# Query, key and value products in three 16-bit passes, one copy and one subtraction moved to GpSimd, new order lists, and products without a reader at both ends

## The reference

```python
x = L0_attn_x                                # (8, 512, 256) float32
mod = (silu(L0_c) @ L0_wmod).reshape(8, 6, 1, -1)
sa, ca, ga, sb, cb, gb = ...                 # ga, gb: absolute value at least 0.25
h = layernorm(x) * (1 + ca) + sa
qkv = h @ w_qkv                              # 16 heads of 16
q = elu(rope(q) * 16**-0.25) + 1;  k the same
kv += k[:, None] * v;  ks += k               # scan over the 512 positions
out = (q @ kv) / max(q . ks, 1e-6)
x = x + ga * (out @ w_out)
h = layernorm(x) * (1 + cb) + sb
probs = softmax(h @ router_w.T);  the top 2 of 8 experts, weights made to sum to 1
x = x + gb * sum_e cw_e * (gelu(h @ w1_e) @ w2_e)
```

## Time and profile before

| | us |
|---|---|
| median of three runs (761.94 to 768.41) | 763.54 |
| the profiled execution | 765.42 |
| its span | 763.6 |
| busy in the span: PE, DVE, ACT, POOL | 710.8, 624.6, 567.0, 500.7 |
| mean granted TensorE clock | 0.96 |

### The profile page before, as it was taken

One profiled execution on the slowest core, in us unless ns is written; L12 is line 12 of the kernel. 1 busy time (PEld: TensorE's weight loads), 2 busy tenths in 40 slices (PEclk: granted clock), 3 DMA queues, 4 the chain that ended last, 5 costly groups with the idle time before them and its releaser, 6 DMA issues.

```text
span 763.6 us, 24900 instructions
## 1 busy us (share of the span) xinstructions
PE 710.8 (93%) x8105; PEld 545.1 (71%) x8105; DVE 624.6 (82%) x1494; ACT 567.0 (74%) x1108; POOL 500.7 (66%) x535
## 2 busy tenths in 40 slices
...
GB/s 225 133 62 158 116 150 121 137 139 112 140 113 142 115 128 99 50 28 65 56 76 72 71 71 73 71 78 71 78 69 78 68 77 72 76 70 76 70 21 1
DMA packets 52854, 69.26 MB, mean 91 GB/s; under 512 B 8864, under 2 KB 44080, under 8 KB 52736
## 3 DMA queue, kind: packets, MB, share of 16 engines
...
...
## 4 chain that ended last, share of the span: by engine, by line
PE 55%; POOL 19%; issue 13%; DVE 2%; ACT 2%; DMA 1%; POOLq 0%; ACTq 0%; DVEq 0%
PE hidden L1484 17%; PE bank L1502 16%; PE hidden L1486 8%; PE bank L1504 8%; POOL h L902 4%; POOL kst L941 4%; POOL qst L939 3%; PE bank L1319 2%; POOL rstd L895 2%; POOL kst L932 2%; PE bank L1336 2%; POOL am L921 1%; POOL mod_b L987 1%; POOL ra L946 1%; PE hidden L1319 1%
## 5 line engine op out<-in xcount | busy, mean ns | idle before, releaser
L1484 PE MATMUL hidden<-qstT,w1hi_k 128*128 128x256 f16 x1136 | 197.7, 274 | 0.7 <-DVE qstT L782 0.7
L1486 PE MATMUL hidden<-qstT,w1lo_k 128*128 128x128 f16 x1136 | 193.3, 220 | 0.0
L1502 PE MATMUL bank<-w,amhi 128*128 x568 | 188.4, 379 | 0.1
L1504 PE MATMUL bank<-w,amlo 128*128 x568 | 154.8, 273 | 0.0
L1035 POOL DMA_INDIRECT out_dram<-x,si x71 | 115.5, 1627 | 39.5 <-issue 24.6
L818 DVE TENSOR_TENSOR amlo<-am,amhi 128x512 f16<-128x512 f32 x142 | 98.3, 692 | 49.0 <-ACT am L1195 48.6
L1484 PEld LDWEIGHTS hidden<-qstT,w1hi_k 128*128 x1136 | 111.6, 98 | 13.8 <-issue 1.2
L1486 PEld LDWEIGHTS hidden<-qstT,w1lo_k 128*128 x1136 | 111.6, 98 | 0.5 <-issue 0.2
L1336 PE MATMUL bank<-wq,hT 128*128 128x256 f32 (+1 forms) x256 | 99.4, 513 | 4.2 <-DVE hT L550 2.9
L1502 PEld LDWEIGHTS bank<-w,amhi 128*128 128x128 f16 x568 | 55.6, 98 | 59.9 <-issue 0.4
L1048 ACT ACTIVATE feat<-hidden 128x512 f32<-128x512 f32 x71 | 42.4, 597 | 61.9 <-PE hidden L1486 61.9
...
## 6 DMA issues: line engine op xcount, KB each, us to landing
...
```

Source lines behind the costliest of these rows:

```text
L1484: t.matmul(dst.rearrange("p (q n) -> p q n", q=2), w1s[0][k][g][:, w_], both, start=(k == 0), stop=False)
L1486: last = t.matmul(dst[:, P:2 * P], w1s[1][k][g][:, w_], both[:, 0, :], start=False, stop=(k == KT - 1))
L1502: t.matmul(y[:, :], ghi[:, m.p, c_m], w2s[mt // 2][:, bass.ds(w_, 2 * D)], start=(mt == 0), stop=False)
L1504: last = t.matmul(y[:, D:2 * D], glo[:, m.p, c_m], w2s[mt // 2][:, bass.ds(w_, D)], start=False, stop=(mt == MT - 1))
```

## The change

- `product16` makes queries, keys and values of chunks 3 to 31 from 16-bit halves: for each half of the depth, high rows by high weights, high rows by low weights, low rows by high weights, six products in place of two float32 ones. Chunks 0 to 2 (`PLAIN = 3`) still go by float32, from `wq_raw`, which lies in the second half of tiles for expert weights that are filled later.
- New works for that: `wqh` (ACT, two copies of 128x768) and `wql` (DVE, two) split the weights once; `hh` (ACT) and `hl` (POOL) split the rows of each chunk. The weights are scaled by 64 and the tables of the rotation are left as they were: chunks 0 to 2 get the 64 in `rope`, the others lose it in `vhi` and `vlo`. `vlo` is a `scalar_tensor_tensor` now. The tile `hT` exists once, no longer twice.
- `shq` goes from ACT to POOL, and `slo` is one instruction of 128x512 in place of two: both stacks lie in one tile `stacks`, and the quarter low by low is zero, set once.
- `mv`, `rstd` and `nb` exist twice, so `rs` no longer waits for `nb`, `xn` and `xn2` of the step before; `var` is gone.
- All lists are new. `warm` (two products of the identity with itself) stands nine times in PE's step 1 and three times in its step 5, and `fill` (the same, after the last state is read) twenty times in PE's closing list. The closing lists begin at step 26, not 27.

```diff
-Q_SCALE = WS * float(HD ** -0.25)
+Q_SCALE = float(HD ** -0.25)
-ORDER_POOL = (("h2", 6), ("rs", 0), ("wb", 5), ("shk", 2), ("slo", 2), ("xm2", 5), ("R", 1))
+ORDER_POOL = (("h2", 6), ("rs", 0), ("shq", 2), ("shk", 2), ("slo", 2), ("wb", 4), ("hl", 0), ("R", 1), ("xm2", 5))
...
+PLAIN = 3
...
+        wq16 = wq[:, :, :].bitcast(F16).rearrange("p k n -> p (k n)").rearrange("p (k c n) -> p k c n", k=KT, c=2)
...
-        mv = sb("mv", [P, 2, 2])
-        var = sb("var", [P, 2])
-        rstd = sb("rstd", [P, 2])
-        nb = sb("nb", [P, 2])
+        mv = sb("mv", [P, 2, 2, 2])
+        rstd = sb("rstd", [P, 2, 2])
+        nb = sb("nb", [P, 2, 2])
         h = sb("h", [P, D])
-        hT = sb("hT", [P, 2, D])
+        hT = sb("hT", [P, D])
+        h16 = sb("h16", [P, 2, D], F16)
...
+        stacks = sb("stacks", [P, 2 * STACK + 3 * HD], F16)
...
             def steadied(m):
...
-                wait(dve, a_["rs"], m.n)
-                v.tensor_scalar(var[:, :], mv[:, :, 1], LN_EPS, None, ALU.add).then_inc(a_["ve"], 1)
+                wait(dve, a_["xn"], m.n - 1, NC)
+                wait(dve, a_["xn2"], m.n - NORM2 - 1)
+                v.tensor_scalar(rstd[:, m.p, :], mv[:, m.p, :, 1], LN_EPS, None, ALU.add).then_inc(a_["ve"], 1)
...
             def h_modulated(m):
 
                 wait(dve, a_["hT"], m.n + 1)
-                wait(dve, a_["qk"], m.n - 1)
-                wait(dve, a_["v"], m.n - 1)
+                if m.n > PLAIN:
+                    wait(dve, a_["hl"], m.n - PLAIN)
+                else:
+                    wait(dve, a_["qk"], m.n)
+                    wait(dve, a_["v"], m.n)
...
+            def qkv_low(m):
+
+                k = m.n
+                dve.wait_ge(s_wqh, k + 1)
+                v.scalar_tensor_tensor(out=wq16[:, k, 1, :], in0=wq_raw[k], scalar=WS, in1=wq16[:, k, 0, :],
+                                       op0=ALU.mult, op1=ALU.subtract).then_inc(s_wql, 1)
...
             def root(m):
 
                 wait(pool, a_["ve"], m.n + 1)
-                wait(pool, a_["nb"], m.n)
-                wait(pool, a_["xn"], m.n, NC)
-                wait(pool, a_["xn2"], m.n - NORM2)
-                g.tensor_tensor(rstd[:, :], var[:, :], minus_half[:, :], ALU.pow).then_inc(a_["rs"], 1)
+                g.tensor_tensor(rstd[:, m.p, :], rstd[:, m.p, :], minus_half[:, :], ALU.pow).then_inc(a_["rs"], 1)
...
+            def stack_q(m):
+
+                wait(pool, a_["f"], m.n + 1)
+                wait(pool, a_["Tq"], m.n)
+                f = feat[:, :].rearrange("p (q h u d) -> p q h u d", q=2, h=NH, u=1)
+                g.tensor_copy(qst[:, :, 0:3:2, :], f[:, 0].broadcast_to([P, NH, 2, HD])).then_inc(a_["shq"], 1)
...
                 wait(pool, a_["shq"], m.n + 1)
                 wait(pool, a_["shk"], m.n + 1)
-                f = feat[:, :].rearrange("p (q h u d) -> p q h u d", q=2, h=NH, u=1)
-                g.tensor_tensor(qst[:, :, 1:4:2, :], f[:, 0].broadcast_to([P, NH, 2, HD]), qst[:, :, 0:3:2, :],
-                                ALU.subtract)
-                g.tensor_tensor(kst[:, :, 2:4, :], f[:, 1].broadcast_to([P, NH, 2, HD]), kst[:, :, 0:2, :],
-                                ALU.subtract).then_inc(a_["slo"], 1)
+                g.tensor_tensor(lows, feat[:, :].rearrange("p (q h d) -> p q h d", q=2, h=NH), highs, ALU.subtract)\
+                    .then_inc(a_["slo"], 1)
+
+            def h_low16(m):
+                if m.n < PLAIN:
+                    return
+                wait(pool, a_["hh"], m.n - PLAIN + 1)
+                g.tensor_tensor(h16[:, 1, :], hT[:, :], h16[:, 0, :], ALU.subtract).then_inc(a_["hl"], 1)
...
+            def h_high(m):
+                if m.n < PLAIN:
+                    return
+                wait(act, a_["hTe"], m.n + 1)
+                wait(act, a_["qk"], m.n)
+                wait(act, a_["v"], m.n)
+                copy(h16[:, 0, :], hT[:, :]).then_inc(a_["hh"], 1)
...
+            def product16(dst, m, lo):
+
+                for k in range(KT):
+                    hi_, lo_ = (h16[:, c, k * P:(k + 1) * P] for c in range(2))
+                    last = mm3(dst, hi_, lo_, wq16[:, k, 0, lo], wq16[:, k, 1, lo], start=(k == 0), stop=(k == KT - 1))
+                return last
...
+            def without_reader(m):
+
+                wait(pe, a_["sth"], B * (CPB - 1))
+                wait(pe, a_["stl"], B * (CPB - 1))
+                for _ in range(2):
+                    t.matmul(bank[4][:, NH * VW:NH * VW + P], ident[:, :], ident[:, :], start=True, stop=True)
+
+            def kept_running(m):
+
+                for _ in range(2):
+                    t.matmul(bank[3][:, 0:P], ident[:, :], ident[:, :], start=True, stop=True)
```

148 lines of the change are left out of this document (87 added, 61 removed), and 74 rows, old and new, of tables (CLOSING_ACT, CLOSING_DVE, CLOSING_PE, CLOSING_POOL).

## The result

The changed kernel takes 768.38 us (median of 22 runs, 766.90 to 770.35), the kernel before beside it 766.22 (22 runs). The ratio is 1.0036, 95% interval 1.0024 to 1.0048: slower by 0.4%, where 0.65% faster was forecast. The profiled span is 766.0 us against 763.6, and the difference splits as follows. The view is the one of the earlier trace rows, for the same stretches by event: up to `f` of chunk 4, from there to `f` of chunk 31, and the closing.

What follows compares the result with a forecast made beforehand. DVE was taken as the middle's bound, busy 239.56 of 244.9 us. Middle -5.0, opening +1.2 and closing -1.1 sum to -4.9 us, which from the median of 763.54 gives 758.6; range 751 to 768.

Steps and rivals of the forecast that it cites:

- Middle, -5.0: From `f` of chunk 4 to chunk 31, fewer DVE waits save 5.0 us; bounds -7.5 and +1.5.
- a lighter PE and ACT may return half, 2 us: Middle: of DVE's five idle microseconds, 2 us come back because PE and ACT have less work.
- `hl` puts two handovers more between `hTe` and `v`: Middle: POOL's new row split lengthens the way from `hTe` to `v`; named without a time of its own.
- DVE waiting for `hT` in each step: Middle: one of the things the trace would show if the forecast was wrong; no size given.
- my first rival: Middle stays at 9.07 us a step, DVE not the whole bound or waits' gain taken back; 763.6 us, chance 0.26.
- Opening, +1.2: Up to `f` of chunk 4, added weight splitting and products cost 1.2 us; bounds 0 and +3.4.
- Followed along both lists to `f` of chunk 2, it comes some 2.3 us later: Opening: `f` of chunk 2 slips 2.3 us, with 1.1 us of DVE work already done by then.
- The terms for `warm`: Opening, PE: 0.16 us a record, 1.9 us ahead of the transposes, 2.6 ahead of `qk`; `rope` of chunk 0 slips 1.5.
- The bound of +3.4: Opening's worst case: 1.5 us of delay plus 1.9 us of DVE work.
- Closing, -1.1: After `f` of chunk 31: 1.9 us gained earlier, 1.8 lost to `fill` and a transpose, 1.1 returned by the clock at `pj`.
- The slower rival: Middle: POOL instructions land on DVE's `wlo`, taking it from 1.35 to up to 1.80 us each step; 773.8 us, chance 0.11.
- POOL, arriving in them, waits and DVE does not: Middle: a POOL instruction arriving during `wlo`'s two instructions waits, leaving DVE undelayed; no size given.

Runs made afterwards that it cites:

- split_aTe: Changed kernel with ACT's `aTe` copy made in four instructions of 64 columns, not one; ratio to the kernel before 1.0085.
- split_whi: Changed kernel with the first of ACT's two `whi` copies made in four instructions; ratio to the kernel before 1.0064.
- v_twice: Changed kernel with the six 16-bit products of `v` computed twice from chunk 3 on; ratio to the kernel before 1.0233.
- nb_early: Changed kernel with DVE's `nb` of chunk 2 moved ahead of the modulation rows' instructions; ratio to the kernel before 1.0006.
- no_warm: Changed kernel with the twelve `warm` entries removed from PE's opening lists; ratio to the kernel before 1.0049.
- stl_behind_x1: Changed kernel with, in the repeated lists, `sth` behind `aTe` (ACT), `stl` behind `x1` (DVE), `state` behind `v` (PE); ratio to the kernel before 1.0187.

## Why the prediction was wrong

**Middle, -5.0; measured -0.7.** The prices themselves were right: `rs` at 0.70 but for three of 26, `wlo` at 1.28 (1.26 expected), and DVE's busy time fell by 5.3 us. The step that failed is the sentence that gave this to the time: "a lighter PE and ACT may return half, 2 us", with "`hl` puts two handovers more between `hTe` and `v`" costed at nothing. I compared each engine's sum with the step and took DVE as the bound. But `hh` is an instruction of ACT in the middle of its list that waits for DVE, which waits for PE, which waits for ACT's `aTe`: this way is 0.32 us longer than what ACT has to do in between, so a step is ACT's 8.93 us and these 0.32. One of the prediction's own signs of being wrong, DVE waiting for `hT` in each step, is what the trace shows. split_aTe and split_whi show it, v_twice the second way round, by PE's own list. What the ports gave, the circle took; it was my first rival, at 0.26, and its condition ("the longer way from `hTe` to `v` takes what the waits give").

**Opening, +1.2; measured +5.6, some 5.0 as a mean of executions.** The failed step is "Followed along both lists to `f` of chunk 2, it comes some 2.3 us later": it came 6.0 later, at 42.26. The step counted durations along DVE and PE, and overlooked that `nb` of chunk 2 had changed sides with the modulation rows, an instruction of 0.16 us: 2.7 us by nb_early. It also overlooked that `nb` of chunk 0 had gone behind the statistics of chunk 1, for which `xn` and so `hT` waited, and put 1.9 us of `warm` ahead of `hT`, which cost nothing there. The terms for `warm` were too high: a record of it costs less than I took (16 in 1.95 us, 0.12 each, not 0.16), `rope` of chunk 0 came 0.8 us later (14.68, 13.89 before), not 1.5, and that `warm` keeps the clock up, 2.7 us by no_warm, was no term at all. The bound of +3.4 held for what remains behind nb_early, 2.3, whose cause is open.

**Closing, -1.1; measured -2.4.** Right in sign and in its mechanism: `aT` of chunk 31 stood behind `fill`, and the time before that point gained. The clock's part was right: `pj` gives back 1.05 us (2.11 from its start to `x1` before, 1.06 after), where I had 1.1. Mis-sized were `fill` (16 records in 1.95 us, so 0.5 for an entry of four, not 0.64) with the transpose beside it, which cost 1.1 us on the way to `pj` where I had 1.8, and the gain ahead of `at`, 2.4 where I had 1.9; both errors lie on the same side. What I didn't see is that without `fill` the clock stays up in part by itself (`pj` 1.13 to 1.76), so that `fill` costs more than it returns.

**The shared ports.** The slower rival did not happen in the changed kernel, but it did in stl_behind_x1, after three moves meant to help. Against that rival stood "POOL, arriving in them, waits and DVE does not", from a power of 128x2 that waited through both instructions of `wlo`. The product of 128x256 that arrived in the first (193.94) did not: it took 0.77, and the second instruction of `wlo` 1.22. The Trainium skill ("SBUF — State Buffer", Who interferes with whom) has the first to start keep the shared ports; for two long instructions the trace agrees, 0.68 free and 1.22 behind POOL's start. For the small power it does not here either: `f` started 0.20 us behind `rs` (189.33) and took 0.68.
